# Self-attention of a decoder block on one core: token quarters outside, head groups inside, one output projection per token tile

## What is computed

```python
def _L0_attn_ref(x, Wq, bq, Wk, bk, Wv, bv, Wo, bo):
    q = (x @ Wq.T + bq).reshape(b, l, h, hd).transpose(0, 2, 1, 3)
    k = ...; v = ...
    scores = jnp.einsum('bhqd,bhkd->bhqk', q, k) / math.sqrt(hd)
    scores = jnp.where(causal, scores, -jnp.inf)
    att = jax.nn.softmax(scores, axis=-1)
    out = jnp.einsum('bhqk,bhkd->bhqd', att, v)
    return out.transpose(0, 2, 1, 3).reshape(b, l, d) @ Wo.T + bo

x = _layernorm(x + _L0_attn_ref(x, ...))
x = _layernorm(x + _L0_xattn_ref(x, ctx_4096, ctx_4096, mask, ...))
x = _layernorm(x + _L0_ffn_ref(x, ...))
```

## Time and profile before

| | |
|---|---|
| median of 3 runs | 1782.42 us (1780.18 to 1782.51) |
| the profiled execution, its span | 1784.5 us |
| TensorE busy | 1702.5 us, 95% of the span |
| VectorE, ScalarE, GpSimd busy | 1295.5, 915.0, 923.0 us |
| self-attention, first matmul to first matmul of the cross-attention | 11.32 to 325.33 us |

### The profile page before, as it was taken

One profiled execution on the slowest core, in us unless ns is written; L12 is line 12 of the kernel. 1 busy time (PEld: TensorE's weight loads), 2 busy tenths in 40 slices (PEclk: granted clock), 3 DMA queues, 4 the chain that ended last, 5 costly groups with the idle time before them and its releaser, 6 DMA issues. The chain is left out here.

```text
span 1784.5 us, 38613 instructions
## 1 busy us (share of the span) xinstructions
PE 1702.5 (95%) x15285; PEld 977.4 (55%) x15285; DVE 1295.5 (73%) x2102; ACT 915.0 (51%) x1525; POOL 923.0 (52%) x745
## 2 busy tenths in 40 slices
PE   6999999899999999999999999999889999899996
PEld 3666666455555555555555555555555555455553
DVE  4787889788888888888888888888786444344445
ACT  4565667665546555555455555555742333233334
POOL 7643125463646464646455546455643555455544
PEclk9999999999999999999999999999999999999999
DMA  8720020221313122314122222121166778787658
GB/s 251 178 47 22 8 63 3 65 85 36 130 37 107 66 83 78 107 42 132 53 93 74 72 72 95 37 95 48 60 213 209 153 155 221 216 205 153 118 95 295
DMA packets 84991, 190.62 MB, mean 107 GB/s; under 512 B 10768, under 2 KB 29584, under 8 KB 82768
## 3 DMA queue, kind: packets, MB, share of 16 engines
q1 hardware_dynamic: 61152, 129.67, 21.6%
q0 software_dynamic: 23088, 58.37, 16.0%
q10 hardware_dynamic: 576, 0.11, 0.0%
HBM read 124.91 MB, written 63.21 MB: 105 GB/s over the span
## 5 line engine op out<-in xcount | busy, mean ns | idle before, releaser
L288 PE MATMUL bank<-xhl,front_h 128*128 128x512 f16 x704 | 268.8, 382 | 12.4 <-DVEq L68 11.8
L289 PE MATMUL bank<-xhl,front_h 128*128 128x512 f16 x704 | 268.7, 382 | 0.0
L290 PE MATMUL bank<-xhl,front_l 128*128 128x512 f16 x704 | 268.5, 381 | 0.0
L1048 POOL TENSOR_TENSOR xa_xs<-xa_xs,sn 128x512 f32<-128x512 f32 x160 | 232.3, 1452 | 45.8 <-ACT xa_xs L1100 45.8
L1059 POOL TENSOR_TENSOR xa_sc<-xa_sc,xa_rs 128x1024 f32<-128x1024 f32 x32 | 60.9, 1902 | 374.6 <-DVE xa_rs L1316 374.6
L1053 POOL TENSOR_TENSOR xa_rr<-xa_x,xa_xs 128x512 f32<-128x512 f32 x160 | 233.3, 1458 | 12.7 <-DVE xa_x L1211 0.2
L288 PE MATMUL bank<-out_h,xa_oh 128*128 128x512 f16 x512 | 194.1, 379 | 10.3 <-DVE xa_ol L1193 6.6
L1967 POOL DMA_INDIRECT scratch_y<-raw_front,moe_to x79 | 125.3, 1585 | 150.4 <-DVE mo_zl L2021 120.0
L290 PE MATMUL bank<-out_h,xa_ol 128*128 128x512 f16 x512 | 194.0, 379 | 0.0
L289 PE MATMUL bank<-out_l,xa_oh 128*128 128x512 f16 x512 | 194.0, 379 | 0.0
L1099 ACT ACTIVATE xa_xs<-bank 64x512 f32<-64x512 f32 x160 | 95.1, 594 | 130.3 <-PE bank L290 126.6
(11 more groups left out here) (307 smaller groups left out, 4589.0 us busy)
## 6 DMA issues: line engine op xcount, KB each, us to landing
xa_rawc<-in_ew SPq DMA_DIRECT2D x32, 768.0 KB, 5.7
moe_ring<-scratch_w SPq DMA_DIRECT2D x16, 1536.0 KB
scratch_w<-xa_chunk_h SPq DMA_DIRECT2D x32, 384.0 KB, 2.3
scratch_w<-xa_chunk_l SPq DMA_DIRECT2D x32, 384.0 KB, 3.3
raw_front<-in_xwq SPq DMA_DIRECT2D x8, 1024.0 KB, 7.9
raw_out<-in_xwo SPq DMA_DIRECT2D x8, 1024.0 KB, 5.4
scratch_y<-acc SPq DMA_DIRECT2D x6, 1024.0 KB, 8.0
acc<-in_x POOLq DMA_DIRECT2D x4, 1024.0 KB, 10.2
```

The costliest lines, as they stand in the source:

```text
L288: pe.matmul(out_ap, ah, bh, start=start and m == 0, stop=False)
L289: pe.matmul(out_ap, ah, bl, start=False, stop=False)
L290: mm = pe.matmul(out_ap, al, bh, start=False, stop=stop and m == n - 1)
L1048: PO.mark(pool.tensor_tensor(xr, xr, sn[:, :].rearrange("p (a s) -> p a s", a=1) .to_broadcast([P, QT // S, S]), ALU.mult), f"sm{r}", st)
```

## The change

- The outer loop is over quarters and the inner one over groups (`st.i` is the quarter, `st.q` the group, `n` counts the 16 steps). The split weights of all four groups stay in memory: two groups in `front_h`/`front_l`, two in `late_h`/`late_l`. Groups 1 to 3 are split whole in steps 0, 1 and 2 (128x1536 elements), and the output weights whole in step 3 (128x2048), on ScalarE and VectorE.
- The outputs `oh`/`ol` of the steps are kept in 7 slots. The projection of a token tile is taken over all four groups at once, 12 matmuls into one bank (`output`): one tile in each of the steps 5 to 15, tile 11 after the last step, and tiles 12 to 15 at the very end. VectorE then adds one tile per step in place of four.
- Tiles 0 to 7 are normed inside the steps (`statistics` on VectorE, `inverse_root` on GpSimd, `nr` on ScalarE), and turned one step later (four float32 transposes, `tu`). The four transposes of `turn_whole` for quarter 1 and the float16 path for quarter 0 go away; quarters 2 and 3 are turned in the cross-attention as before.
- Scores have the four banks 0 to 3, which keys (0) and queries (1) share; so keys wait for `sb0` and queries for `sb1` of the step before. In a step the 48 matmuls of the values stand in one piece, then the masks of the four pairs, then the scores of pairs 0 and 1, then those of 2 and 3, then `back_pv`, the projection and `back_turn`.
- The mask is written by 16 matmuls of 32 rows and 64 columns of the array (8 with 512 elements, 8 with 256) in place of 4 of 64 rows.
- Values leave their bank through one ScalarE copy (`v32`); the high and low parts are taken from it by GpSimd.
- Inputs come in halves of a quarter, one per step.
- The loading and preparing of the mask input (`bound`) moves into the cross-attention: SyncE issues its two DMAs first there, and GpSimd runs `mask_bound` after its third sum of the first step.
- The first group of cross-attention output weights is split whole by ScalarE and VectorE in step (0, 1), where it was one head of four.

Core of the diff (TensorE's new queue in the self-attention; last, SyncE and GpSimd in the cross-attention):

```diff
-                    def back_out(st):
-                        pe.wait_ge(DV.sem, DV.value("ol", st))
-                        for t in range(TQ):
-                            PE.mark(three_pass(pe, o[:, :], [(oh[:, tok], ol[:, tok], wo_h, wo_l)]), f"w{t}", st)
+                    def output(tile, bank_, name, st):
+                        c, tok = tile // TQ, tokens(tile % TQ)
+                        PE.mark(three_pass(pe, bank_[:, :], [(oh[:, slot(c * NG + g), tok], ol[:, slot(c * NG + g), tok],
+                                                              wo_h[:, g, :], wo_l[:, g, :]) for g in range(NG)]), name, st)
...
+                        for h in range(2):
+                            for b2 in range(2):
+                                for j in J4:
+                                    r, q = slice(32 * j, 32 * j + 32), slice(64 * b2, 64 * b2 + 64)
+                                    pe.matmul(SB[j][q, :].rearrange("p (a c) -> p a c", c=S)[:, :, 32 * h:S], identb[r, h, :],
+                                              maskb[r, h, :, 32 * h:S], start=h == 0, stop=False, skip_group_check=True)
+                        for js in ((0, 1), (2, 3)):
...
+                    def step(n):
+                        st = step_of(n)
+                        if n:
+                            pe.wait_ge(DV.sem, DV.value("sb0", st, 1))
+                        feature_major("k", st, 0, () if n else ("pt0", "pt1"))
+                        if n:
+                            back_p(st, (0, 1))
+                            pe.wait_ge(DV.sem, DV.value("sb1", st, 1))
+                        feature_major("q", st, 1, () if n else ("pt2", "pt3", "tu"))
+                        if n:
+                            back_p(st, (2, 3), ("tu",) if turned is None else ())
...
+                        values(st)
...
+                        scores(st, () if n else ("pv0", "pv1", "w", "oT"))
+                        if n:
+                            back_pv(st, ("w",) if tile is None else ())
+                            if tile is not None:
+                                output(tile, home["w"], "w", st)
+                            back_turn(st)
...
+                    back_p(done, (0, 1))
+                    pe.wait_ge(DV.sem, DV.value("sb3", done, 1))
+                    back_p(done, (2, 3))
+                    output(STEPS - W_LAG, home["w"], "w", done)
+                    back_pv(done)
+                    next_keys(pe)
+                    back_turn(done)
+                    next_values(pe)
+                    for t in range(TQ):
+                        output(3 * TQ + t, last_home[t], f"w{t}", done)
...
+                    for h in range(2):
+                        sp.dma_start(bound[64 * h:64 * h + 64, :, :], maskf.rearrange("b q k -> q b k")).then_inc(s_mask, 16)
...
                             PO.mark(pool.tensor_tensor(rr[r % 2][:, :], x0[r % 3][:, :], xs[r % 3][:, :], ALU.add), f"ra{r}", st)
+                            if first and (q, r) == (0, 2):
+                                mask_bound(pool)
```

More of the change, by code:

```diff
@@ L326, in self_attention @@
                 at = b("at", [P, TQ, P])
[L327 to L331 removed]
+                oh, ol = b("oh", [P, SLOTS, QT], F16), b("ol", [P, SLOTS, QT], F16)
@@ L734, in _ @@
-                    ln.wait(dve, ln.AC, "lower_h")
-                    ln.DV.mark(dve.scalar_tensor_tensor(front_l[:, lower], raw_front[:, lower], WS, front_h[:, lower], ALU.mult,
-                                                        ALU.subtract), "lower_l", ln.now)
-                    ln.inverse(dve, 1, 1)
+                        below_most(st, 3)
+                    for n in range(STEPS):
+                        step(n)
+                    done = Step(None, 0)
+                    back_lo(done, 0)
```

768 lines of the change are left out of this document (365 added, 403 removed).

## The result

| | before | changed |
|---|---|---|
| median | 1781.98 us (4 runs, 1780.18 to 1782.51) | 1805.75 us (4 runs, 1804.21 to 1806.20) |
| ratio, 95% interval | | 1.0134 (1.0120 to 1.0148) |
| span of the profiled execution | 1784.5 us | 1803.8 us |
| first matmul of the self-attention, of the cross-attention | 11.32, 325.33 us | 9.91, 334.06 us |

The account below looks back on a forecast made before the run. TensorE's queue was taken to bound the kernel. From the profiled span of 1784.5 us, -14.6 - 5.6 - 6.8 + 3 + 7.5 + 9.5 = -7.0 gave 1777.5, a median of 1775.4 us; range 1761 to 1789.

Parts of the forecast that it names:

- What bounds the kernel: Whole kernel: TensorE, busy 95% of the span; time changes where its queue gets shorter or stands still.
- Steps 5 to 15, 16.22 us of work: Self-attention steps with a projection: 16.22 us each in place of 17.87, the 1.13 us wait gone; -14.6 us in all.
- rival (a): Masks in the self-attention steps do not overlap: 1780 us at four at a time, 1791 at two; 12%.
- Step 0, -5.6: First self-attention step: four banks take all scores, so 11.2 us to the next keys in place of 16.77.
- Steps 1 to 4, -6.8: Self-attention steps without projection: 64.7 us against 71.5, with TensorE waiting for a normalisation made late by weight splitting.
- irregular idle time, +3: Self-attention idle times without a wait, and the lower clock: 12 us where there were 9, 4 to 20 possible.
- rival (b): Instruction gaps become the rule in the self-attention: two more than counted, 6.3 us each, make 1788 us; 15%.
- The waits of 2.4 to 3.5 us: Self-attention steps 1 to 3: TensorE waits this long each for the late normalisation; 1.3 us in step 4.
- End of the self-attention, +7.5: Last step's end to the cross-attention's first matmul: 25.3 us in place of 17.9, with four tiles' projections bare.
- Start of the cross-attention, +9.5: GpSimd's mask preparation, hidden before, moves everything behind it by 9.1 us; waiting for the mask transfers adds 0.4.
- The gap by tiling mode: Between pieces of different shape TensorE loses 0.09 to 0.12 us: three gaps per step where there were seven.

Follow-up runs that it names:

- e1: Changed kernel with the values of two of the four token tiles put between scores and probability products: 1797.4 us, ratio 1.0099 to the kernel before.
- e10: e9 with the values back in one piece in front of the scores: 1781.9 us, ratio 0.9998 to the kernel before.
- e9: e8 with rows of x loaded one 256 KB tile per step in steps 0 to 14, not 1 MB in steps 0 to 3: 1777.8 us, 0.9971.
- e3: Changed kernel with the rows of x and bias loaded in steps 3-4, 7-8, 11-12 and 13-14, not 0 to 4: 1802.5 us, ratio 1.0115.
- e6: Changed kernel with the output bias added by GpSimd, one tile per step, in place of four 1 MB accumulating transfers: 1791.4 us, ratio 1.0038.
- b1: Kernel before the change, with the output bias added by GpSimd in steps 6 to 13 in place of accumulating transfers: 1782.2 us, ratio 0.9997.
- e11: e9 with three value tiles before the scores in step 0 and the mask input in four pieces, one per step: 1773.8 us, ratio 0.9952.
- e4: Changed kernel with the self-attention's end reordered: tile 11's projection first, then all transposes, next keys, products: 1800.1 us, ratio 1.0112.
- e7: Changed kernel with the edits of e1, e3 and e4, the mask input in two pieces and the square-root table loaded early: 1803.1 us, ratio 1.0100.
- e8: Changed kernel with the edits of e1, e4 and e6, the mask input in two pieces and the square-root table loaded early: 1779.8 us, ratio 0.9987.

## Why the prediction was wrong

The span came out 26.3 us above the forecast (1803.8 against 1777.5). By its own steps:

1. *What bounds the kernel.* Right: TensorE's queue, its work and where it stands still.
2. *Steps 5 to 15, 16.22 us of work.* Right where nothing disturbs: steps 9 and 11 take 16.59 and 16.79 us, forecast 16.66 with the turning. The waits for VectorE are gone as laid out, nothing took their place, and the masks were 0.35 us (forecast 0.33), so rival (a) was wrong.
3. *Step 0, -5.6.* 27.98 - 15.05 = 12.93 us where 11.2 was forecast, 1.7 more, on ScalarE; TensorE itself began the keys of step 1 at 23.43 us, forecast 24.9. The stage began 1.4 us earlier, which I had not counted.
4. *Steps 1 to 4, -6.8,* **and** *irregular idle time, +3.* **This is the step that failed.** From the keys of step 1 to those of step 15 my terms give 64.7 + 10 x 16.22 + 8 x 0.44 + 12 = 242.4 us; it took 264.1, so 21.7 of the 26.3 us are here. I had seen the gaps and the clock behind them, and costed them by how often they had come (two long ones in 14 steps) instead of by what makes them. The sentence "as many instructions are fetched as before and the small matmuls stand closer together, so I expect such gaps again" has the cause in it, and then 3 us as its price. The row of small matmuls in one step went from 146 (scores of two pairs, products) to 208; the "320 now, 200 before" of rival (b) fits neither count. With blocks of 126 matmuls both rows always hold the end of one. What grew is the chance that a whole block lies in the row and is used up in about 2 us: 82 of 126 positions now, 20 of 126 before (an estimate from the counts alone). e1 and e10 show that the row's length does it where transfers are few: 6.6 us in steps 6 to 14 by e1, 4.8 by e10 against e9. e3, e6, e9 and the gap that is left in b1 show that a transfer at that moment makes a gap of 1 us one of 3. The waits of 2.4 to 3.5 us that I had laid out for steps 1 to 3 came as 0.9 us. In step 3 that is because TensorE had stood before: without a gap in front it is 2.47 us in e3 and e10. In steps 1 and 2 it is 0.9 to 1.4 us in every run, so there the layout was too dear. Steps 1 to 4 took 83.0 us by all this, forecast 64.7; in e11, with 2.1 us of gaps, they take 68.1.
5. *Rival (b)* was the right mechanism, with the right price of one gap (2.85 + 3.5 us), but it counted two more gaps and stopped at 1788; in steps 1 to 5 alone there are six of 1.9 to 3.4 us. Its 15% and the range's upper end came from that count.
6. *End of the self-attention, +7.5.* With step 15 it was 9.2 us longer, forecast 5.9. The 3.3 us between are the clock behind the two waits. e4 and e11 had it back with the waits unchanged in sum, e7 and e10 with the same order of the end had not, so the new order is not shown to be the reason.
7. *Start of the cross-attention, +9.5.* +10.6 (19.3 less 8.7 at the stage's first matmul). Right in size, partly for other reasons: the transfers cost 0.33 us (forecast 0.4), and the lower clock is hidden by the next wait, as forecast: 8.5 us were lost, 5.1 in e1 and e4, and the work behind comes at the same time. The table load and VectorE's 4.12 us were not seen; so the size is right partly by luck. The 10.5 us are all there 82.7 us after the stage's first matmul and no more are added up to 834 us after it.

At two places a rule had been weighed. The Trainium skill (Runtime: NRT & Kernel Launch, Instruction fetch mechanics) has instructions coming in blocks of 256. The grid of 256 instructions in both traces agrees with that; its "mostly hidden" does not hold here, with 24 us of gaps in 324. The gap by tiling mode (TensorEngine Tiling (Array Packing), Key Properties) fits the 16.59 us of step 9, but no run took such a gap away by itself, so it stays unproven.

That waits alone lower the clock stands in the traces (e9 above, and the end of the self-attention here, 3.4 of the 24.0 us). Open is why the same wait does so in one execution and not in another.

## What to carry to other kernels

A rearrangement that only shortens TensorE's waits by putting small matmuls together should be costed by instructions per microsecond: count from the trace where the gaps called "issue" fall, find their spacing in instructions, and ask for each place of that spacing how long the block before it lasts. Put large matmuls between rows of small ones, cut transfers that run beside such rows into pieces (256 KB did little harm here, 1 MB did), and give every gap or wait the clock's loss behind it as well. And when work is moved to a new place, look what ran on that engine for other reasons (a table, an idle time) where it was.

## What the runs showed of the hardware beyond that

- At the gaps, a block of instructions is there 2.2 to 4.0 us after the one before it was begun when few transfers run, and 4.8 to 6.9 us, once 10.1, when the DMA share in that time is 0.44 or more (end of gap less start of the matmul 126 places ahead, in the changed kernel, e3, e6 and e10).
- Eight pieces of the array (32 rows by 64 columns) run 16 masks in 0.35 us.
- One and the same wait of 3.6 us behind tile 11's projection cost no clock in e4 and e11, 1.7 us in e8 and e9, 3.4 us in e7 and e10 (one profile each). The clock's price of a wait is not fixed by its length.
- VectorE's float16 low part, from two operands in SBUF, takes 3.8 to 4.1 us in place of 0.7 to 1.1 when it begins beside the first of GpSimd's two operations on the mask (128x1536 or 128x2048); operations with an operand in a bank kept their 0.69 beside it. In e8 the subtraction of the maximum, both operands in SBUF, took 2.05 in place of 0.69 there. Beside the second operation the same subtraction took 0.69.
